# Reordering the hand-over from a first scan unit to the loop behind it, in a one-core hybrid attention, expert and state-space kernel

## The reference, cut to what matters

```python
def fp_step(y_prev):
    x_tilde = (x - y_prev) @ W_mix.T + y_prev
    bc = _shift1(y_prev) @ W_bc.T
    Bt = bc_normalize(B0 + bc[..., :D_STATE])
    Ct = bc_normalize(C0 + bc[..., D_STATE:])
    y = _selective_scan(x_tilde, delta, A, Bt, Ct, D)
    return layer_norm(y)
...
y_star = jax.lax.fori_loop(0, FP_ITERS, lambda i, y: y + STEP * (fp_step(y) - y), y0)
y = fp_step(y_star)
# in _selective_scan, for each token:
h = jnp.exp(dt_t[:, :, None] * A) * h + (dt_t * u_t)[:, :, None] * b_t[:, None, :]
y = jnp.einsum('bdn,bn->bd', h, c_t) + D * u_t
```

## Time and profile before

| | |
|---|---|
| median of 3 runs | 10301.96 us (10301.13 to 10309.9) |
| the profiled execution | 10288.07 us, its span 10285.8 us |
| VectorE busy | 8862.1 us, 86% of the span |
| TensorE busy (matmul) | 9253.0 us, 90% |
| ScalarE busy | 7235.6 us, 70% |
| GpSimd busy | 6118.4 us, 59% |

### The profile page before, as it was taken

The page is one execution under the profiler, slowest core; times in us unless marked ns, Lnnn a source line. Parts: engine busy times, 40 slices in busy tenths (PEclk is TensorE's granted clock), DMA queues, the critical chain, the costliest instruction groups (busy, mean ns, idle before and its releaser), DMA issues.

```text
span 10285.8 us, 259086 instructions
## 1 busy us (share of the span) xinstructions
PE 9253.0 (90%) x88474; PEld 6391.3 (62%) x88474; DVE 8862.1 (86%) x16781; ACT 7235.6 (70%) x15052; POOL 6118.4 (59%) x4900
## 2 busy tenths in 40 slices
PE   7989899898998989989899899999989999899988
PEld 4656656566565665656656566565665656656566
DVE  6988979789797897978979799797997979879798
ACT  5867768677686776857768576685866858668586
POOL 1936829377293772927729277392763928639286
PEclk9999999999999999999999999999999999999999
DMA  0000000000000000000000000000000000000000
GB/s 22 0 3 1 2 3 0 3 1 2 3 0 3 1 2 3 0 3 1 2 3 0 3 1 2 3 0 3 1 2 3 0 3 1 2 3 0 3 1 3
DMA packets 648478, 23.66 MB, mean 2 GB/s; under 512 B 629185, under 2 KB 647250, under 8 KB 647506
## 3 DMA queue, kind: packets, MB, share of 16 engines
q1 hardware_dynamic: 647890, 16.11, 3.7%
HBM read 9.40 MB, written 4.19 MB: 1 GB/s over the span
## 4 chain that ended last, share of the span: by engine, by line
DVE 28%; PE 23%; issue 18%; POOL 17%; ACT 11%; DVEq 1%; POOLq 1%; DMA 0%; SPq 0%; ACTq 0%
POOL work L1714 16%; DVE work L1605 11%; DVE work L1595 6%; PE ps L605 4%; ACT scan_in L1099 4%; PE ps L595 4%; PE ps L590 3%; PE ps L534 3%; PE ps L522 2%; DVE stats L1225 1%; ACT da L985 1%; ACT yscT L1132 1%; DVE scan_in L1509 1%; POOL skip_u L1687 1%; PE ps L802 1%
## 5 line engine op out<-in xcount | busy, mean ns | idle before, releaser
L1714 POOL TENSOR_TENSOR work<-work,crep 128x512 f32<-128x512 f32 x4608 | 5765.1, 1277 | 4093.7 <-DVE work L1544 3590.7
L1099 ACT ACTIVATE scan_in<-du,bcn 128x256 f32<-128x256 f32 x8832 | 3690.6, 497 | 69.6 <-PE ps L812 36.9
L1605 DVE TENSOR_TENSOR_SCAN work<-da,hend,ps 128x256 f32<-128x256 f32 x4608 | 3028.0, 725 | 57.8 <-PE ps L812 48.7
L812 PE MATMUL ps<-w_ident,scan_in 128*128 128x128 f32 x18432 | 2455.3, 278 | 275.6 <-ACT scan_in L1099 147.0
L812 PEld LDWEIGHTS ps<-w_ident,scan_in 128*128 128x128 f32 x18432 | 2018.9, 142 | 873.6 <-DVE work L1605 324.6
L1595 DVE TENSOR_TENSOR_SCAN work<-da,ps 128x512 f32<-128x512 f32 x2048 | 2353.4, 1201 | 38.8
L802 PE MATMUL ps<-work,w_sel 128*32 128x256 f32 x17792 | 1408.7, 390 | 276.5 <-POOL work L1714 275.5
L1020 ACT ACTIVATE work<-ps,w_gate_b 128x512 f32<-128x512 f32 x512 | 349.6, 686 | 824.7 <-PE ps L590 684.4
L802 PEld LDWEIGHTS ps<-work,w_sel 128*32 128x32 f32 x17792 | 375.3, 108 | 756.7 <-POOL work L1714 541.3
L1336 DVE TENSOR_REDUCE smax<-ps 128x1 f32<-128x512 f32 x1024 | 656.9, 685 | 162.0 <-PE ps L499 158.0
L985 ACT ACTIVATE da<-ps 128x512 f32<-128x512 f32 x1024 | 555.3, 606 | 147.3 <-PE ps L522 140.4
(11 more groups left out here) (205 smaller groups left out, 12083.1 us busy)
## 6 DMA issues: line engine op xcount, KB each, us to landing
hend<-work SPq DMA_DIRECT2D x2304, 1.0 KB, 1.8
x_in<-in_x SPq DMA_DIRECT2D x17, 256.0 KB, 2.8
out<-work SPq DMA_DIRECT2D x16, 256.0 KB
gate_w<-in_gate_w SPq DMA_DIRECT2D x1, 1024.0 KB, 5.0
up_w<-in_up_w SPq DMA_DIRECT2D x1, 1024.0 KB, 7.1
down_w<-in_down_w SPq DMA_DIRECT2D x1, 1024.0 KB, 9.1
w_w_zy<-in_w_zy SPq DMA_DIRECT2D x1, 256.0 KB
work<-in_w_mix SPq DMA_DIRECT2D x1, 256.0 KB
```

The costliest lines, as they stand in the source:

```text
L812: mm = eng.transpose(ps[:, bank, c:c + P], scan_in[:, m, tb, 2 * j + s].rearrange("p k c -> p (k c)"), ident[:])
L1099: ins = eng.activation(scan_in[:, m, tb, :, k, :], du[:, hf, tb, :].rearrange("p (e c) -> p e c", c=GC), ACT.Copy, scale=bcn[:, hf, tb, 0, ...
L1605: ins = eng.tensor_tensor_scan(hst[:, p % NHID, half], da[:, 1, 2 * p + s, :], ps[:, RING[p % 4], half], hend[:, 2 * p + s:2 * p + s + 1], ...
L1714: eng.tensor_tensor(prod[:, to, :].rearrange("p (s t) -> p s t", s=2), hst[:, p % NHID, :].rearrange("p (s t) -> p s t", s=2), crep[:, hf, ...
```

## The change

Five things are moved; no work is added or dropped.

1. ScalarE's fill for the second half waits for the transposes of the twelfth piece in the order (0, 3), the last of m = 0, and not for those of all 16.
2. The last replica of delta is issued behind piece 7 together with the one before it, and no longer behind piece 8.
3. The C replicas of the second half come in two parts: rows 0 and 1 (bank 6) behind the transposes of piece 14, after a wait for its decays, and rows 2 and 3 (bank 7) behind those of piece 15. The fourth sum moves from behind piece 13 to behind piece 14, after the first part.
4. One of the two D products (the first half's) moves to GpSimd's place behind its product of piece 7.
5. `LATE_AT` begins with 0 in place of -1: in every unit of the loop, and in the one behind it, the first late sum comes behind the transposes of piece 0 and not ahead of them.

```diff
--- before.py
+++ after.py
@@ -66,14 +66,14 @@
 FIRST_BANK = (0, 1, 2) * 4 + RING
 FIRST_PROD = (2, 0, 6, 4, 3, 1, 7, 5, 2, 3, 6, 7, 0, 1, 6, 7)
 FIRST_SUMS = (0, 2, 4, 1, 3)
-FIRST_SUM_AT = (7, 8, 9, 13)
-FIRST_REP_AT = (3, 4, 7, 8)
+FIRST_SUM_AT = (7, 8, 9, 14)
+FIRST_REP_AT = (3, 4, 7, 7)
 REP_BANK = (5, 6, 7, 4)
 BATCH = 2
 NB = NP // BATCH
 LAG = 3
 SUM_AT = (3, 6, 7, 11, 15)
-LATE_AT = (-1, 3, 3)
+LATE_AT = (0, 3, 3)
 
 
 class Place:
@@ -691,13 +691,16 @@
                     scan_input(at, m, j, FIRST_BANK[p])
                     if p == 2:
                         keep_busy(4, 3)
-                    if p in FIRST_REP_AT:
-                        cb = NK + FIRST_REP_AT.index(p)
-                        eng.wait_ge(da_ready.sem, da_ready.count(at, NM * (cb // 2 - 1)))
-                        repeat_delta(at, cb)
+                    for k, behind in enumerate(FIRST_REP_AT):
+                        if p == behind:
+                            eng.wait_ge(da_ready.sem, da_ready.count(at, NM * ((NK + k) // 2 - 1)))
+                            repeat_delta(at, NK + k)
+                    if p == NP - 2:
+                        eng.wait_ge(da_ready.sem, da_ready.count(at, NP - 1))
+                        repeat_c(at, 1, 6, (0, 1))
                     if p in FIRST_SUM_AT:
                         first_sum(at, FIRST_SUM_AT.index(p))
-                front_c(at, 1, 1)
+                repeat_c(at, 1, 6, (2, 3))
                 first_sum(at, 4)
 
             def first_sum(at, k):
@@ -756,9 +759,9 @@
                     eng.wait_ge(u_copied.sem, u_copied.count(at, kf + 1))
                 repeat_c(at, hf, 6)
 
-            def repeat_c(at, hf, bank):
-
-                for m in range(NM):
+            def repeat_c(at, hf, bank, rows=range(NM)):
+
+                for m in rows:
                     for tb in range(HB):
                         c = m % 2 * TH + tb * P
                         for k in range(NK):
@@ -767,7 +770,8 @@
                                 ps[GC * k:GC * (k + 1), bank + m // 2, c:c + P],
                                 bcn[:, hf, tb, 1, n:n + 1].broadcast_to([P, GC]), ident[:],
                                 start=(m % 2 == 0 and tb == 0), stop=(m % 2 == 1 and tb == HB - 1))
-                mm.then_inc(c_rep.sem, c_rep.up(at))
+                if rows[-1] == NM - 1:
+                    mm.then_inc(c_rep.sem, c_rep.up(at))
 
             def back_d(at, hf, kb):
 
@@ -1188,7 +1192,7 @@
                 attention(at)
                 mixture(at)
                 ssm_inputs(at)
-                eng.wait_ge(b_done.sem, b_done.count(at, NP))
+                eng.wait_ge(b_done.sem, b_done.count(at, FIRST.index((0, QP - 1)) + 1))
                 fill(at, 1, 0, 0)
                 fill(at, 1, 0, 1).then_inc(filled.sem, filled.up(at))
                 eng.wait_ge(c_rep.sem, c_rep.count(at, 2))
@@ -1702,12 +1706,17 @@
                         k = FIRST_SUMS.index(2 * FIRST[last][0] + FIRST[last][1] // 2)
                         eng.wait_ge(nsummed.sem, nsummed.count(at, k + 1))
                     product(at, 0, p, m, FIRST_PROD[p])
-                for hf in range(2):
-                    eng.wait_ge(x_mixed_a.sem, x_mixed_a.count(at, 1))
-                    eng.tensor_tensor(
-                        skip_u[:, hf], x_mixed[:, hf * HB:(hf + 1) * HB, :],
-                        w["skip"][:].rearrange("p (o c) -> p o c", o=1).broadcast_to([P, HB, DI]),
-                        ALU.mult).then_inc(skip_done.sem, skip_done.up(at))
+                    if p == NP // 2 - 1:
+                        first_skip(at, 0)
+                first_skip(at, 1)
+
+            def first_skip(at, hf):
+
+                eng.wait_ge(x_mixed_a.sem, x_mixed_a.count(at, 1))
+                eng.tensor_tensor(
+                    skip_u[:, hf], x_mixed[:, hf * HB:(hf + 1) * HB, :],
+                    w["skip"][:].rearrange("p (o c) -> p o c", o=1).broadcast_to([P, HB, DI]),
+                    ALU.mult).then_inc(skip_done.sem, skip_done.up(at))
 
             def product(at, hf, p, m, to):
```

## The result

| | before | after |
|---|---|---|
| median of 5 runs, us | 10301.96 (10289.36 to 10309.9) | 10254.5 (10248.78 to 10257.38) |
| ratio, 95% interval | | 0.9955 (0.9942 to 0.9969) |
| profiled execution, span, us | 10285.8 | 10252.2 |
| first scan to the loop's second unit, 16 stretches | 782.90 | 737.43 |
| the rest of the loop, 16 x | 5511.47 | 5512.67 |

The change makes the kernel 47 us faster by the medians, where 22 were forecast. The last four rows split that: -45.5, +1.2, +13.5 and -2.8.

A forecast was written before the change was run, and what follows sets the result against it. VectorE was taken to set the loop's pace, so only its idle time around the first unit could be gained. -41 (head) + 5 (clock) + 14 (late sum) = -22 us, from 10302 to 10280 us, range 10256 to 10308.

The forecast's parts named there:

- the term of part 5: First-half loop units: the moved late sum costs VectorE 0.11 us each, 14 us lost over 128 units.
- the late sum costs nothing: Rival, chance 0.18: the moved late sum is free in the loop, 10266 us; 0.02 us of slack decides.
- The clock in the tail: TensorE's C replicas, sum and transposes before the loop: low clock in a third of 0 to 14 us, 5 us lost.
- 14 us lost by it: Tail before the loop: by the rule, transposes leave the clock low in most elements, losing 14 us and not 5.
- The row that the prediction set against the rule: Earlier trace: 33 records, nearly all transposes, at granted clock 1.00 from 2099.65 to 2103.05, said to stay there behind them.
- Parts 1 and 3, the tail: Hand-over to the loop: first loop scan 21.9 us behind the first, stretch 46.4 against 48.93, 41 us over 16.
- Part 2: Delta replicas in the first unit: ScalarE's remaining decays come 1.15 us earlier, scan 8 gains 1.1 us.
- Part 4: GpSimd before product 8: the D product fills its wait, products 8 to 15 stay within 0.13 us.
- the head gives little: Rival, chance 0.17: GpSimd's D product delays the fifth sum and loop by 1 us; 16 of 41 us go, 10296 us.
- the head and its clock: Hand-over to the loop: 41 us gained, 5 us lost to the low clock, -36 together.
- its own best case: All terms at their best, with a first loop unit of 24.01 and nothing for clock and late sum: -48 us.
- the 10 us for the clock's phase: Whole kernel: another start of each element shifts where the low clock falls, some 10 us either way.

The follow-up runs named there:

- a1: Kernel before with only the late sum moved behind piece 0: 10303.4 us, ratio 1.0002 to before.
- g1: Kernel after with three idle transposes (0.33 us) added behind piece 0 in every loop unit: 10324.16 us, ratio 1.0025 to before.
- g2: Kernel after with eight idle transposes (0.88 us) added behind piece 0 in every loop unit: 10480.3 us, one run.
- e1: Kernel after with all 64 C replicas behind piece 15 again, fourth sum still behind piece 14: 10263.8 us, ratio 0.9966 to before.
- e2: Kernel after with the fourth sum back ahead of piece 14, C replicas still in halves: 10286.88 us, ratio 0.9989 to before.
- d1: Kernel after with the last delta replicas behind piece 8 again: 10273.5 us, ratio 0.9974 to before.
- f1: Kernel before with 14 idle transposes added between scan 11 and the fourth sum: 10301.31 us, ratio 0.9998 to before.
- c1: Kernel after with ScalarE's fill waiting for all 16 pieces again: 10276.05 us, ratio 0.9978 to before.
- b1: Kernel after with both D products behind the first unit's last product again: 10253.24 us, ratio 0.9952 to before.
- b3: Kernel after with one D product ahead of GpSimd's first product, once scan_in is filled, the other behind the last: 10229.6 us, ratio 0.9934 to before.

## Why the prediction was wrong, by its steps

**The step that failed is the term of part 5**, "I charge 0.11 us of VectorE per first-half unit: 128 units, 14 us lost". The runs show nothing of that size: the rest of the loop grew by 1.2 us in after and by 0.3 in a1, first-half units by 0.02. Two sizes in it were off. The last late sum comes 1.61 us behind scan 0 (2343.73 and 0.45 for the sum ahead of it, against 2342.57) where it came 1.56 behind, 0.05 later and not 0.13, and piece 4's transposes come only 0.02 later. And the prediction read the 0.25 us between their end and scan 4 as needed "nearly all" by VectorE. In g1 and g2, where scan 4 does wait for them, it starts 0.18 us behind their end. In before it follows VectorE's own moments, so there was slack of 0.08 us where the step took 0.02; 0.06 are left in after (g1). The mechanism is real: 0.33 us put in there cost 0.27. The rival "the late sum costs nothing" was the right one; it named 0.02 us of slack as what decides, and then the likelier side was chosen wrongly.

**The clock in the tail** was charged with 5 us and cost nothing: 1.00 in all 16 stretches. The prediction saw the idle time before the fourth sum shrink from 1.99 to about 1.2 us; it is 0.78. With 1.77 us there (e1) and 2.88 (e2) the clock falls in all 16. The length of this wait is not all that decides: in d1 the clock falls in eight elements about 15.5 us behind the first scan, with no single wait above 0.81 us in the 4 us before. The full clock is also a part of the gain that the sum doesn't name. The two elements of before at 1.00 took 48.12 us; against them the order alone gives 2.03 us per element, 32 us of the 45.5, and the other 13 are the low clock that after no longer has.

The prediction weighed the Trainium skill's rule (TensorE: Matmul & The Clock Gate, Part 4), that transposes don't count for the clock as matmuls do, and worked out 14 us lost by it. The measured 0 goes against that. So does f1, with less force: the replicas behind its 14 transposes have the full clock in 16 of 16 elements, in before in two, but in 13 of the 16 the clock was low just before. Whether these are transposes of the kind that the page means, no row shows. The row that the prediction set against the rule doesn't carry what it says: the clock did not stay at 1.00 behind the 32 transposes of the earlier trace rows. It was 0.50 from 2106.6 us on, behind 2.27 us in which TensorE was idle (us, busy of PE, PEld, DVE, ACT and POOL, granted clock, DMA):

```profile
2106.60:2109.90 3.30, 3.30 (x70) 3.30 (x65) 3.20 (x7) 3.09 (x9) 0.00 (x0) 0.50 0.03 7
```

**Parts 1 and 3, the tail** were right in their order and nearly in size. The fifth sum waits for GpSimd, piece 0 is right behind it, the loop's first scan comes 21.74 us behind the first (21.9 forecast), and the loop's first unit takes 24.35 (24.46 forecast). These two make 0.27 us per element, 4 us of 16. c1, e1 and e2 bear out each of the three edits: undoing one costs 33 to 47 us in the stretch, a part of it in each by the low clock, and so they don't add, each is needed for the others.

**Part 2** went as worked out for ScalarE: its wait is 0.18 us in place of 1.34, and the decays come 1.15 us earlier. Scan 8 comes 0.92 us earlier and not 1.1, since VectorE's own scan 7 ends last ahead of it and not the transposes. Its worth at the loop is small, 0.36 us per element at the full clock (d1).

**Part 4** was right in that the D product fits into GpSimd's wait for scan 8: product 8 starts 12.73 us behind the first scan, where it started at 12.64, and the fifth sum comes at 20.22, where 20.4 was forecast. That rules out the rival "the head gives little", though half of its condition came true: scan 8 gained less than 1.1 us. But b1 shows that without part 4 the stretch would be as short. The prediction didn't look for this; it didn't ask which engine the hand-over would wait for afterwards.

**The sum.** On the profiled executions the head and its clock gave -45.5 for -36, part 5 +1.2 for +14, and what no edit touches +10.7 (13.5 less 2.8) for 0: -34 for -22. The other 14 of the 47 us come from the profiled execution of before having been below its median, which the prediction saw, taking the change off the median. So of the 25 us between -22 and -47, 13 are part 5, 9.5 the head and its clock, and 3 the balance of two things that no edit made, +10.7 and -14; that these nearly cancel is luck. The result is 1.5 us below the range. The range's lower end was cut at -46, where its own best case and the 10 us for the clock's phase reached to -58.

**What stays open** is the unchanged part. The 15 windows from the last unit to the next first scan, in after, its shortest and its longest:

```profile
3140.29:3385.15 244.86, 172.21 (x415) 0.99 0.01 4
...
5687.88:5938.00 250.12, 172.24 (x415) 0.96 0.01 3
...
sum 3708.20, DVE 2584.84; mean DVE 172.32
```

VectorE does the same 172.2 us in both, and the window at 0.96 is 5.3 us longer than that at 0.99. The sum over 15 went from 3686 us (e1) to 3717 (d1), of two kernels whose edits change nothing in it. It goes with the granted clock; what sets where the clock falls in an element was not found, and no run here steered it. For this reason b3's last 13 us over after, and the exact -47, can't be put down to an edit.

## What to carry to other kernels

When an engine's idle times are to be filled, first ask which engine will bound the stretch afterwards: here it became GpSimd's queue, and moving one of its products mattered only once it went into time in which GpSimd itself had nothing to do, beside an instruction that doesn't contend with it. Chained edits are tested by undoing each one: three of these cost 33 to 47 us each when taken away, where all five together gained 45. Before a delay is charged to an engine, look at what ends last ahead of its next instruction: at scan 4 it was VectorE's own work, and the 14 us charged there were not lost. Measure by the stretch that an edit touches, in all its repetitions, because the untouched stretches of this kernel moved the total by as much as an edit did.

## What was not expected of the hardware

- A D product on GpSimd beside VectorE's two-input products: these went from 1.22 and 1.23 us to 2.27 and 2.18, and two D products together from 2.54 to 3.47. Beside a scan with an input in PSUM: 1.28 us, and the scan unslowed.
- With 14 idle transposes ahead of them the C replicas had the full clock in 16 of 16 elements, without them in two of 16. The low level showed up elsewhere, from about 15.5 us behind the first scan on, in 13 of 16, where before had it in six.
- The same 172.2 us of VectorE work took 244.86 to 250.12 us, with the granted clock at 0.99 and 0.96.
